# Attention scores on TensorE: each piece as two products of 64x64 tiles instead of one of 64x128

## What is computed

```
x = x + expert(x)            # a 512x512 matrix and bias of 16, chosen per sequence
x = x + W x + adapter(x)     # rank 16, one of 8 adapters per sequence
x = x + attention(x)         # 8 query heads, 4 key/value groups of 64, window of 256 keys, paged cache
x = x + mix(x)               # 64x64 over the tokens, one of 8 per sequence
```

```
q, k, v = x Wq, x Wk, x Wv;  q, k = rope(rms(q)), rope(rms(k))
k_blocks, v_blocks = written at the positions of the new tokens
scores = einsum('bghtd,bgsd->bghts', qg, k_all) * SCALE
scores = where(allowed, scores, -inf)       # kpos <= pos and kpos > pos - 256
p = softmax(scores)
o = einsum('bghts,bgsd->bghtd', p, v_all);  out = o Wo
```

## Time and profile before

| | us |
|---|---|
| runs | 952.81, 953.42, 951.57; median 952.81 |
| span of the profiled execution | 948.6 |
| median of the runs less that span (no separate time of the profiled execution is given) | 4.2 |
| TensorE matmul busy | 907.5 (96%) |
| TensorE weight loads busy | 660.8 (70%) |
| VectorE, ScalarE, GpSimd busy | 651.1, 444.3, 522.3 |
| phase two, from the first scores to the last | 521.9 to 928.9 |
| scores (L775), busy | 88.6, 768 matmuls |

### The profile page before, as it was taken

How to read it: one execution, slowest core, us unless ns; L and a number is a source line. 1 busy time by engine, 2 the same in 40 slices (tenths; PEclk the granted TensorE clock), 3 DMA queues, 4 the chain that set the end, 5 groups by cost and what they waited for, 6 DMA issues and landing times.

```text
span 948.6 us, 23332 instructions
## 1 busy us (share of the span) xinstructions
PE 907.5 (96%) x6477; PEld 660.8 (70%) x6477; DVE 651.1 (69%) x1853; ACT 444.3 (47%) x1190; POOL 522.3 (55%) x502
## 2 busy tenths in 40 slices
PE   5789999999999999999997899999999999999997
PEld 3456666766666667666676777877777887787785
DVE  5345545667768774556754678777878877888875
ACT  2333333333333333333322566666666666666663
POOL 2136455464564657855556666566565665656530
PEclk9799999999999999999998799999999999999999
DMA  9978988778788787887844566666666676567741
GB/s 295 265 230 282 330 308 290 252 261 289 247 282 276 244 291 255 271 295 247 284 159 152 183 188 203 199 210 186 198 197 212 200 225 203 181 209 212 221 135 46
DMA packets 100413, 218.51 MB, mean 230 GB/s; under 512 B 30187, under 2 KB 36168, under 8 KB 92178
## 3 DMA queue, kind: packets, MB, share of 16 engines
q1 hardware_dynamic: 66290, 145.27, 47.0%
q0 software_dynamic: 25088, 57.74, 20.5%
q10 hardware_dynamic: 8992, 15.00, 4.9%
HBM read 210.39 MB, written 33.86 MB: 257 GB/s over the span
## 4 chain that ended last, share of the span: by engine, by line
PE 51%; POOL 18%; issue 15%; DMA 7%; SPq 4%; DVE 2%; ACT 1%; ACTq 1%; POOLq 0%; DVEq 0%
PE banks L823 9%; PE banks L775 9%; PE banks L811 7%; PE banks L798 6%; POOL rms L471 5%; DMA ring<-in_rope 5%; PE banks L752 4%; PE banks L859 3%; POOL ring L475 3%; POOL x_in L461 3%; PE banks L816 3%; POOL q_rot L480 2%; PE banks L753 1%; PE banks L791 1%; POOL ring L482 1%
## 5 line engine op out<-in xcount | busy, mean ns | idle before, releaser
L561 POOL DMA_INDIRECT ring<-new_rows,idx x128 | 129.4, 1011 | 82.5 <-PE banks L775 40.3
L471 POOL TENSOR_TENSOR rms<-ss,neg_half 128x12 f32<-128x12 f32 x31 | 70.8, 2284 | 185.4 <-DVE ss L1259 185.4
L992 ACT ACTIVATE big<-big,neg_max 128x320 f32<-128x320 f32 x256 | 141.4, 554 | 3.1 <-DVE neg_max L1317 2.7
L1317 DVE CUSTOM_DVE_ANT_0 big<-banks,mask 128x320 f32<-128x320 f32 x256 | 114.6, 486 | 27.4 <-PE banks L775 26.0
L602 PE MATMUL banks<-ring 128*64 128x512 f32 x512 | 117.8, 601 | 0.9 <-DMA ring<-in_w 0.9
L982 ACT ACTIVATE kt<-banks 128x384 f32<-128x384 f32 x128 | 61.8, 483 | 97.5 <-PE banks L753 97.5
L775 PE MATMUL banks<-kt,q_in 64*128 64x128 f32 (+2 forms) x768 | 88.6, 364 | 1.3 <-ACT kt L982 1.3
L550 POOL DMA_INDIRECT ring<-new_rows,idx x64 | 61.7, 965 | 47.0 <-PE banks L798 42.7
L1354 DVE TENSOR_SCALAR big<-big,recip 128x320 f32<-128x320 f32 x256 | 85.5, 396 | 2.3
L775 PEld LDWEIGHTS banks<-kt,q_in 64*128 64x128 f32 x768 | 74.4, 189 | 14.4 <-issue 8.4
L811 PEld LDWEIGHTS banks<-pt,ring 128*64 128x64 f32 x1024 | 55.4, 136 | 38.1 <-DVE pt L1299 25.4
(11 more groups left out here) (177 smaller groups left out, 1989.0 us busy)
## 6 DMA issues: line engine op xcount, KB each, us to landing
ring<-in_w SPq DMA_DIRECT2D x62, 1024.0 KB, 7.5
ring<-in_xt SPq DMA_DIRECT2D x32, 256.0 KB, 2.7
x_in<-in_x SPq DMA_DIRECT2D x32, 256.0 KB, 5.8
bias_in<-in_b SPq DMA_DIRECT2D x64, 128.0 KB, 6.4
x_dram<-x SPq DMA_DIRECT2D x32, 256.0 KB, 6.9
q_dram<-q_t ACTq DMA_DIRECT2D x32, 256.0 KB, 5.7
new_rows<-kv_out SPq DMA_DIRECT2D x32, 256.0 KB, 6.7
q_in<-q_dram SPq DMA_DIRECT2D x32, 256.0 KB, 2.7
```

The lines of the kernel that those rows point to most:

```text
L471: nc.gpsimd.tensor_tensor(rms[:, s, :], ss[:, s, :], neg_half[:, :], ALU.pow).then_inc(rms_ready, 1)
L561: pool.indirect_dma_start(out=kv[:, s, c, :], out_offset=None, in_=new_rows, in_offset=bass.IndirectOffsetOnAxis(ap=idx[:, b, 1 + c:2 + c] ...
L992: nc.scalar.activation(prob[:, s % 2, PLACE[g] * NK:(PLACE[g] + 1) * NK], sm[:, s % 2, g, :], ACT.Exp, bias=neg_max[:, s % 2, g:g + 1], sc ...
L1317: V.tensor_tensor_reduce(sm[:, s % 2, g, :], ps_s[g], mask[:, s % 2, k0:k0 + NK], 1.0, 3.0e38, ALU.add, ALU.min, accum_out=neg_max[:, s % ...
```

## The change

Each piece is made by two products, one for each head's 64 queries: the stationary operand is 64 columns wide, and the output goes to PSUM partitions 0 to 63 or 64 to 127. The streamed keys are the same for both. The semaphores rise with the last product of a piece. The waits for `kt_ready` and `s_shared` become `wait_alone`, for which TensorE gets a counter.

```diff
-        waits_passed = {"pool": sem("pool_waits_passed"), "dve": sem("dve_waits_passed")}
+        waits_passed = {"pool": sem("pool_waits_passed"), "dve": sem("dve_waits_passed"), "pe": sem("pe_waits_passed")}
...
-                    pe.wait_ge(kt_ready, 2 * b + 2)
+                    wait_alone(pe, "pe", kt_ready, 2 * b + 2)
 
                     def piece(g, n0, n1):
                         r0, k0 = HD * (g % 2), T * (1 - PLACE[g] % 2)
-                        return nc.tensor.matmul(banks[:, S0[g] + n0:S0[g] + n1], q_in[r0:r0 + HD, s % 4, g // 2, :],
-                                                kt[r0:r0 + HD, s % 2, g // 2, k0 + n0:k0 + n1], start=True, stop=True)
+                        for h in range(2):
+                            t0, t1 = T * h, T * h + T
+                            last = nc.tensor.matmul(banks[t0:t1, S0[g] + n0:S0[g] + n1], q_in[r0:r0 + HD, s % 4, g // 2, t0:t1],
+                                                    kt[r0:r0 + HD, s % 2, g // 2, k0 + n0:k0 + n1], start=True, stop=True)
+                        return last
...
-                    pe.wait_ge(s_shared, b + 1)
+                    wait_alone(pe, "pe", s_shared, b + 1)
                     piece(3, 0, P).then_inc(s_done, 1)
```

## The result

The changed kernel takes 946.0 us (median of 5 runs, 944.17 to 947.71) against 952.8 before (950.05 to 953.56): ratio 0.9938, 95% interval 0.9921 to 0.9954, so 4.4 to 7.5 us faster. By the ratio the gain is 5.9 us; the two medians happen to lie 6.8 apart. The forecast was 946.0.

What follows compares the result with a forecast made beforehand. Phase two was taken as bound by two tied loops, TensorE's order and ScalarE/VectorE's run; 0.19 per odd batch plus 0.04 makes 0.23 a pair, x 30 = 6.9 us, giving 946.0 us, range 942.8 to 951.5.

Steps and rivals of the forecast that it cites:

- Columns and issue: Scores on TensorE: twelve 64x64 products stream in 1.09 us like six 64x128; issuing 24 instructions costs 0 to 0.03, taken as 0.
- two tiles abreast: Rival at the scores: only two tiles run at once, 1.09 us more a batch, 1023 us; chance 0.04.
- a starved queue: Rival at the scores: instructions can't be issued fast enough, 0.25 us more a batch, 969 us; chance 0.02.
- the two rules that the prediction cites from the Trainium skill: Matmuls start and end in strict program order (1023 us); about 62 ns sequencer time per matmul without hardware decode (978 us).
- The shape change that goes: Between L816 and the scores: same shape lets scores stream straight behind, 1.47 instead of 1.66, saving 0.19 us per odd batch.
- odd batch: One of two alternating kinds; the even one's step also holds the Wo projection's second half and the L859 product.
- The even batch's 0.09: Even scores, after key copy L982: load at 702.12 and stream sooner, 0.09 us earlier on TensorE.
- L811's 0.07: Values load behind several waits, 0.07 us after ScalarE's end; taken as the handover from key copy to even scores.
- The 0.04 of ScalarE's loop: Even batch: ScalarE's first exponential starts earlier because the key copy does, 0.03 to 0.08 us, taken as 0.04 a pair.
- Two loops: TensorE's order and a ScalarE/VectorE run from odd scores to even L999: odd savings shorten both, even savings only TensorE's.
- The two loops tie: At the even values products (L811), TensorE and ScalarE's copy L999 are both ready at 707.62, so both loops are equally long.
- The waits: Two split-off waits per batch, at kt_ready and s_shared: cost 0 to 0.02 us, without emptying TensorE.

Runs made afterwards that it cites:

- own_first: Changed kernel with the values' two groups swapped, 64x64 group first, so a change of shape again stands ahead of the scores: 952.4 us, ratio 0.9994.
- keys_early3_wide: Kernel before (64x128 products), ScalarE copying keys before the last exponential in odd steps, transposed probabilities before the fourth in even steps: 954.6 us, ratio 1.0022.
- even_only: Changed kernel with 64x64 products in even batches alone, 64x128 in odd ones: 952.4 us, ratio 1.0002.
- odd_only: Changed kernel with 64x64 products in odd batches alone, 64x128 in even ones: 945.2 us, ratio 0.9924.
- early3_wide: Kernel before, with ScalarE's two copies of transposed probabilities ahead of the fourth exponential in even steps: 951.2 us, ratio 0.9988.
- waits_only: Kernel before, 64x128 products kept, only the waits for kt_ready and s_shared split off: 952.9 us, ratio 1.0003.
- keys_first: Changed kernel, with ScalarE's second key copy ahead of the last exponential in odd steps: 956.9 us, ratio 1.0047.
- early3: Changed kernel, with ScalarE's two copies of transposed probabilities ahead of the fourth exponential in even steps: 944.0 us, ratio 0.9912.
- sum_sooner: Changed kernel; keys copied before the last exponential (odd steps), probabilities before the fourth, VectorE's sum x3 before the fourth mask (even): 940.9 us, ratio 0.9882.

## Why the prediction was right

*Columns and issue.* Right. Twelve products of 64x64 cost what six of 64x128 did; the odd stretch from L819's load to L752's is 1.46, forecast 1.47. The rivals of two tiles abreast and of a starved queue are out: 24 matmuls pass within 697.19 - 695.89 = 1.30 us, 54 ns each with start and emptying in it. With them go the two rules that the prediction cites from the Trainium skill, as far as this kernel is concerned: products on different tiles don't wait for each other in program order, and 62 ns a matmul is not what bounds here. Whether hardware decode was on, no run shows.

*The shape change that goes.* Right in kind and size: 0.20 an odd batch, forecast 0.19. own_first shows the mechanism by putting the change of shape back, and keys_early3_wide shows that ready keys alone don't do it.

*The even batch's 0.09.* Wrong in size: it measured 0.01 (1.67 to 1.66). The term that failed is the handover behind the split-off wait, taken as 0.07; it is 0.11 in the changed kernel, in even_only and in odd_only, which puts the load just where the emptying had put it. The rest of the 0.09 was to come from a shorter uncovered load, 0.04. That came to 0.01 or 0.02: from the scores' load to L752's it is 703.18 - 701.91 = 1.27 after, 1.29 before, and 1.24 in own_first's odd batch, whose keys are ready long before. Behind the split-off wait the first matmul starts 0.03 after its load (701.94 against 701.91). That the wait is the cause is shown by batch 8, the only one from 8 on in which the kernel before waits for the copy and not for the emptying. There it hands over in 0.05, as in early3_wide; waits_only, with the same products, takes 574.80 - 574.69 = 0.11:

```profile
574.21 0.48 ACT L982 ACTIVATE kt<-banks 128x384 f32<-128x384 f32 x1
...
574.80 0.22 PEld L775 LDWEIGHTS banks<-kt,q_in 64*128 64x128 f32 x2 [0.24 <-issue]
```

The nearest row, L811's 0.07, was the wrong one. It stands behind a wait instruction of its own too, which in the trace holds the wait for ScalarE's copy (L809 now; L271 is the one of `wait_alone`):

```profile
L809 PEldq EVENT_SEMAPHORE  x64: 486/493/1270, 533.9 to 931.9; - x64
L271 PEldq EVENT_SEMAPHORE  x96: 51/51/51, 575.0 to 874.0; - x96
```

Why the one costs 0.07 and the other 0.11 isn't shown. L809's is under way for 0.49 us or more before the load, L271's for 0.05.

*The 0.04 of ScalarE's loop.* Wrong for the same reason: it measured 0.01, which these traces can't tell from nothing. From VectorE's first mask to ScalarE's first exponential it was 704.51 - 703.89 = 0.62 and is 0.61. VectorE after:

```profile
703.64 0.49 DVE L1320 CUSTOM_DVE_ANT_0 big<-banks,mask 128x320 f32<-128x320 f32 x1
```

So a pair gained 0.19, not 0.23; 30 x 0.19 = 5.7 us, where 6.9 was forecast, within the interval of 4.4 to 7.5. That the median fell on 946.0 exactly is luck: the two medians lie 6.8 apart, about 1 us more than ratio and pairs give.

*Two loops.* Right that time saved in odd steps shortens both and in even steps only one (odd_only, even_only; keys_first). "The two loops tie" was off by 0.04: ScalarE's was the longer, as early3_wide shows. TensorE's own way from L859's load to L811's is 1.06 (early3), not the 1.07 that 0.00085 us a column gave, and the 0.03 in L811's own stretch had been overlooked.

*The waits.* Right that they don't empty TensorE and cost next to nothing (0.01 a pair) where the array empties anyway (waits_only). Not right that they cost at most 0.02: behind a semaphore that rises last it is 0.06 (0.11 against 0.05, batch 8). 64x64 products with plain waits weren't tried, so what the even batches would bring without that cost stays open. With keys that are ready early they bring the odd batches' 0.2 (sum_sooner).

## What to carry to other kernels

List the tile shape of each group of products in TensorE's order: here the change of shape that went was worth 0.2 us, emptying and uncovered load together, so giving two neighbours one shape can pay even if it doubles the instructions. It pays only where the operands are ready in time; look at the last handover ahead of the group, and treat time saved on TensorE as saved only if the loop through the other engines gets shorter too. When an edit moves a wait, look for it again one group further on, as with the sum for L862.

## What was not expected of the hardware

- A wait that stands as an instruction of its own ahead of a group delays it: 0.11 us from the end of ScalarE's copy to the load (waits_only, batch 8), where a wait on the load itself took 0.05 (same batch of the kernel before).
- Four tiles of 64x64 stay abreast over long streams too, up to 320 columns and six instructions a tile, with no loss that shows against two of 64x128. The prediction had counted on it, but only from the two short rounds of L816.
